# A Mamba block with a mixture of experts on one core: eight of 32 products with C on VectorE, a rearranged prologue, unneeded matmuls behind the loop

## The reference

```python
def _selective_scan(x, dt, Bm, Cm, A, D):
    dA = jnp.exp(dt[..., None] * A)
    dBx = (dt * x)[..., None] * Bm[:, :, None, :]
    def step(h, inputs):
        dA_t, dBx_t, C_t = inputs
        h = dA_t * h + dBx_t
        y = jnp.einsum('bdn,bn->bd', h, C_t)
        return (h, y)
    ...
    return jnp.swapaxes(ys, 0, 1) + x * D[None, None, :]

def _mamba_dir(h, in_proj_w, conv_w, conv_b, x_proj_w, dt_proj_w, dt_proj_b, A_log, D, out_proj_w):
    xz = h @ in_proj_w.T
    x, z = (xz[..., :D_INNER], xz[..., D_INNER:])
    x = jax.nn.silu(_causal_depthwise_conv(x, conv_w, conv_b))
    x_dbl = x @ x_proj_w.T
    dt = jax.nn.softplus(x_dbl[..., :DT_RANK] @ dt_proj_w.T + dt_proj_b)
    ...
    y = _selective_scan(x, dt, Bm, Cm, A, D)
    return (y * jax.nn.silu(z)) @ out_proj_w.T
...
x = x + _L0_attn_ref(_L0_cond_ref(x, cond_8, ...), ...)       # forward and reversed direction
x = x + _L0_ffn_ref(_L0_cond2_ref(x, cond_8, ...), ...)       # top 2 of 8 experts, hidden size 1024
```

## Time and profile before

| | us |
|---|---|
| median of 3 runs | 1420.53 (1418.15 to 1420.72) |
| the profiled execution | 1421.41 |
| its span, first to last instruction | 1419.6 |
| prologue, up to DVE's first scan | 46.9 |
| loop, up to DVE's last gates | 46.9 to 936.3 |
| behind the loop, up to the first expert matmul | 936.3 to 985.4 |
| experts | 985.4 to about 1405 |

### The profile page before, as it was taken

One profiled execution on the slowest core, in us unless ns is written; L12 is line 12 of the kernel. 1 busy time (PEld: TensorE's weight loads), 2 busy tenths in 40 slices (PEclk: granted clock), 3 DMA queues, 4 the chain that ended last, 5 costly groups with the idle time before them and its releaser, 6 DMA issues. The chain is left out here.

```text
span 1419.6 us, 16570 instructions
## 1 busy us (share of the span) xinstructions
PE 1309.1 (92%) x5272; PEld 782.0 (55%) x5272; DVE 948.1 (67%) x1164; ACT 715.8 (50%) x1263; POOL 963.3 (68%) x508
## 2 busy tenths in 40 slices
PE   7898999899998889899897888899999999999997
PEld 3343333343433333333343333346999999999996
DVE  3798999999999999999999999963111111111110
ACT  3887876687776576777677564401111111111111
POOL 1898999999999999999999999824122222222211
PEclk9999999999999999999999999987999999999999
DMA  5554555554555454555555554507889888888882
GB/s 181 187 164 133 177 170 158 165 164 164 164 179 178 147 175 153 169 182 166 170 178 178 172 179 148 186 5 268 305 322 317 319 308 324 313 311 321 321 316 45
DMA packets 105497, 290.33 MB, mean 205 GB/s; under 512 B 9649, under 2 KB 19506, under 8 KB 89922
## 3 DMA queue, kind: packets, MB, share of 16 engines
q1 hardware_dynamic: 95762, 271.17, 54.8%
q0 software_dynamic: 9648, 18.09, 6.3%
HBM read 271.41 MB, written 9.96 MB: 198 GB/s over the span
## 5 line engine op out<-in xcount | busy, mean ns | idle before, releaser
L433 PE MATMUL ps_y<-arena,ident 128*128 128x512 f32 x1024 | 501.9, 621 | 58.1 <-POOL arena L1147 46.1
L1147 POOL TENSOR_TENSOR arena<-arena 128x1024 f32<-128x1024 f32 x184 | 438.4, 2392 | 37.4 <-DVE arena L892 21.6
L433 PEld LDWEIGHTS ps_y<-arena,ident 128*128 128x128 f32 x1024 | 191.6, 196 | 330.2 <-issue 212.3
L1131 POOL TENSOR_TENSOR arena<-arena 128x1024 f32<-128x1024 f32 x128 | 305.3, 2386 | 6.3 <-issue 4.2
L700 ACT ACTIVATE ps_de<-arena,An 128x512 f32<-128x512 f32 x256 | 176.4, 689 | 237.3 <-DVE arena L889 236.4
L1197 POOL DMA_INDIRECT out_x<-arena x39 | 61.8, 1584 | 319.4 <-ACT arena L830 285.1
L876 DVE TENSOR_TENSOR ps_u<-ps_du,arena 128x512 f32<-128x512 f32 x256 | 178.7, 698 | 25.6 <-DVE arena L903 11.2
L1098 DVE TENSOR_TENSOR arena<-ps_du,arena 128x512 f32<-128x512 f32 x39 | 27.0, 692 | 232.9 <-PE ps_du L585 232.9
L700 ACT ACTIVATE arena<-arena,An 128x512 f32<-128x512 f32 x256 | 181.1, 707 | 0.0
L889 DVE TENSOR_TENSOR_SCAN arena<-ps_de,hlast,arena 128x512 f32<-128x512 f32 x128 | 163.1, 1274 | 0.2 <-ACT arena L700 0.2
L889 DVE TENSOR_TENSOR_SCAN arena<-ps_de,arena 128x512 f32<-128x512 f32 x128 | 155.3, 1214 | 6.6 <-ACT arena L700 3.7
(11 more groups left out here) (213 smaller groups left out, 1508.2 us busy)
## 6 DMA issues: line engine op xcount, KB each, us to landing
arena<-bc_scratch SPq DMA_DIRECT2D x256, 512.0 KB, 4.6
arena<-in_W SPq DMA_DIRECT2D x117, 1024.0 KB, 8.1
arena<-arena POOLq DMA_DIRECT2D x15, 512.0 KB, 4.6
arena<-in_xT SPq DMA_DIRECT2D x2, 1024.0 KB, 5.1
arena<-in_w2c SPq DMA_DIRECT2D x1, 2048.0 KB, 8.6
arena<-in_xT SPq DMA_DIRECT2D x4, 512.0 KB, 6.1
X_scratch<-stg SPq DMA_DIRECT2D x12, 128.0 KB, 4.8
out_x<-stg SPq DMA_DIRECT2D x12, 128.0 KB, 5.1
```

The source lines that it names most:

```text
L433: t = e.matmul(Y[j][:, :], ident[:, :], hc[:, i % NP, j, :], start=False, stop=(n == 15))
L1131: e.tensor_tensor(uA[:, turn % 2, :, :], duA.rearrange("p (o t) -> p o t", o=1).to_broadcast([128, 2, TH]), ring[:, turn % NR, 0, :, :], A ...
L1147: e.tensor_tensor(hc[:, i % NP, :, :], hh[:, i % NH, :, :], c, ALU.mult).then_inc(gp_hc, 1)
```

## The change

- **OWN** has eight entries in place of nine, evenly four apart, all at odd units.
- **Prologue.** PE does five matmuls on zeros (128x256, into a free bank) before the first real one. DVE writes the second of the two X tiles, ACT the first. ACT takes exp(A_log) before the step width in place of behind its exp, does ln of the second tile first (`first_ln`), and makes the convolution's diagonals behind the second unit's decays in place of ahead of the first's. DVE adds dt's first tile, POOL the second. POOL's first u is cut in two halves with a semaphore each, so that DVE's first scan waits for one half. DVE's first `second_weights` stands behind its first u.
- **End of the loop.** PE does the first half of the second output block ahead of the last two adds in place of behind them.
- **Behind it.** One unneeded matmul of 512 columns ahead of the logits, one of 256 behind each of the four, one of 512 behind these; four in place of three ahead of the mask matmuls, six in place of four behind them.

```diff
-OWN = (3, 7, 10, 14, 17, 21, 24, 28, 31)
+OWN = (3, 7, 11, 15, 19, 23, 27, 31)
...
         ac_dc = sem("dc")
+        dv_dt, gp_u0 = sem("ddt"), sem("gu0")
         ac_dgD, pe_D, ac_ev = (sem(n) for n in ("dgD", "D", "ev"))
...
             if k < 2:
-                e.wait_ge(gp_dt, k + 1)
+                e.wait_ge(gp_dt if k else dv_dt, 1)
             else:
...
+            e.wait_ge(gp_dz, 1)
+            for _ in range(5):
+                e.matmul(PS[7][:, 0:C], xp[:, 0, PAD:PAD + 128], xp[:, 0, PAD:PAD + C], start=True, stop=True)
             e.wait_ge(l_w0, W0)
...
                     side_work(i)
+                if i == NU:
+                    out_block(1, 0, 1, both_side, (0, 1))
                 if i >= LAG:
...
-            out_block(1, 0, 1, both_side, (0, 1))
             for k in (2, 3):
...
                         t.then_inc(full[2 + c], 1)
+            def warm(n, p=7, w=2):
+                for _ in range(n):
+                    e.matmul(PS[p][:, 0:w * C], ident[:, :], opT[:, 0:w, :].rearrange("p k o -> p (k o)"), start=True,
+                             stop=True)
+            for p in (6, 7):
+                e.wait_ge(freed[p], turns[p])
+            warm(1)
             for i in range(4):
...
                 e.matmul(PS[p][:, 0:E], ones_r, bgr, start=False, stop=True).then_inc(full[p], 1)
-            def warm(n):
-                for _ in range(n):
-                    e.matmul(PS[5][:, :], ident[:, :], opT[:, 0:2, :].rearrange("p k o -> p (k o)"), start=True,
-                             stop=True)
+                warm(1, w=1)
+            warm(1)
...
                 e.wait_ge(freed[p], turns[p])
-            warm(3)
+            warm(4, 5)
             e.wait_ge(gp_rw, 1)
...
             t.then_inc(pe_inv, 1)
-            warm(4)
+            warm(6, 5)
...
                     e.activation(sc1[:, j, :], sc1[:, j, :], ACT.Exp, scale=-1.0).then_inc(ac_se, 1)
+            def first_ln():
+                e.wait_ge(ac_se, 2)
+                for j in (1, 0):
+                    e.activation(sc1[:, j, :], sc1[:, j, :], ACT.Ln, bias=1.0).then_inc(ac_ln, 1)
...
             e.wait_ge(l_x0, WX)
-            x1(0, 0)
+            for m in range(2):
+                is_full(e, ("x1", 0, m, 0))
+            p = place["x1", 0, 0, 0][0]
+            e.activation(X[0][:, 0, HB[0]], PS[p][:, :], ACT.Identity, bias=bb[:, 0:1]).then_inc(freed[p], 1)
             e.wait_ge(l_w, W1)
...
             x_rows(0, 0)
+            e.activation(An[:, :, :, :], Al[:, :, :, :], ACT.Exp).then_inc(ac_A, 1)
             for m in range(2):
...
             step_exp(0, 0, 0)
-            e.activation(An[:, :, :, :], Al[:, :, :, :], ACT.Exp).then_inc(ac_A, 1)
-            step_ln(0, 0, 0)
-            for m in range(2):
-                conv_diag(0, m)
+            first_ln()
             e.wait_ge(dv_An, 1)
...
                 decay(i)
+                if i == 1:
+                    for m in range(2):
+                        conv_diag(0, m)
                 if i >= 2 and unit(i - 2)[1] == 0:
...
                 e.wait_ge(ac_dA, i + 1)
-                e.wait_ge(gp_u, i // 2 + 1)
+                if i == 0:
+                    e.wait_ge(gp_u0, 1)
+                else:
+                    e.wait_ge(gp_u, i // 2 + 1)
                 if i >= NH:
...
                                 ALU.add).then_inc(dv_wm, 1)
+            e.wait_ge(l_x0, WX)
+            p = is_full(e, ("x1", 0, 1, 0))
+            e.tensor_scalar(X[0][:, 1, HB[0]], PS[p][:, :], bb[:, 1:2], None, ALU.add).then_inc(freed[p], 1)
             for m in range(4):
...
                     first_conv(m, k)
-            second_weights(0)
             e.wait_ge(ac_A, 1)
             e.tensor_scalar(An[:, :, :, :], An[:, :, :, :], -1.0, None, ALU.mult).then_inc(dv_An, 1)
+            e.wait_ge(ac_sp, 1)
+            e.wait_ge(ac_ln, 2)
+            e.tensor_tensor(dt[:, 0, :], dt[:, 0, :], sc1[:, 0, :], ALU.add).then_inc(dv_dt, 1)
             for p in range(2, 4):
...
                 u(i)
+                if i == 0:
+                    second_weights(0)
                 scans(i)
...
         def _(e):
-            def first_width(m):
-                e.wait_ge(ac_sp, m + 1)
-                e.wait_ge(ac_ln, m + 1)
-                e.tensor_tensor(dt[:, m, :], dt[:, m, :], sc1[:, m, :], ALU.add).then_inc(gp_dt, 1)
...
                     e.wait_ge(dv_sA, 2 * turn - 2)
+                if turn == 0:
+                    for j, done in enumerate((gp_u0, gp_u)):
+                        e.tensor_tensor(uA[:, 0, j, :], duA, ring[:, 0, 0, j, :], ALU.mult).then_inc(done, 1)
+                    return
                 e.tensor_tensor(uA[:, turn % 2, :, :], duA.rearrange("p (o t) -> p o t", o=1).to_broadcast([128, 2, TH]),
...
-            for m in range(2):
-                first_width(m)
+            e.wait_ge(ac_sp, 2)
+            e.wait_ge(ac_ln, 1)
+            e.tensor_tensor(dt[:, 1, :], dt[:, 1, :], sc1[:, 1, :], ALU.add).then_inc(gp_dt, 1)
             u(0)
```

## The result

The change takes 1405.65 us, median of four runs (1401.53, 1403.74, 1407.56, 1408.77), against 1420.22 us before (four runs, 1418.15 to 1420.72): a ratio of 0.9895, 95% interval 0.9877 to 0.9912. The profiled execution of the change is the one of 1403.74 us (span 1401.9), 17.7 us under the profiled one of before. The forecast was 1400 us, with a range of 1395 to 1411. The trace of the change is thus of an execution 1.9 us under its median.

The account below looks back on a forecast made before the run. DVE was taken to bound the loop, with POOL close behind. From the profiled execution, 1421.4 - 3.0 - 2.8 - 7.3 - 7.9 = 1400.4 us, 1399.5 against the median, stated as 1400; range 1395 to 1411 us.

Parts of the forecast that it names:

- rival 1: Behind the loop: PE's clock falls all the same among the logits, +0.4 in place of -7.9 us; 1408.7 us, chance 0.28.
- First part: Prologue up to the convolution's start: early matmuls raise PE's clock, bias writes run side by side; -3.0 us, bounds -0.6 to -3.6.
- rival 3: Prologue: the early matmuls do not raise PE's clock; 1402.8 us, chance 0.06.
- Second part: Prologue up to DVE's u of unit 1: less work before the first scan; -2.8 us, bounds -1.5 to -4.
- DVE's add beside POOL's: Prologue: DVE's add and du take turns with POOL's; first scan some 0.6 us later than side by side, still in time.
- Loop, -7.3 forecast: Loop: DVE drops its ninth product in eight groups of 32 units, 8 x 0.91 = -7.3 us.
- together 0: Loop: POOL's bumps, about +3 us, and DVE's shorter waits for PE's adds, about -3 us, cancel.
- the +3 for POOL: Loop: POOL's added products, +8.6 us in all, sometimes make DVE wait; about +3 us, bounds 0 to +8.6.
- The -3 for the adds: Loop: DVE's 8.1 us of waits for PE's adds shrink, unit 21 being owned no more; about -3 us, bounds -8.1 to 0.
- Rival 4: Loop: owned unit 19 of every 32 waits 4.1 us for the first add after Y is emptied; 1433 us, chance 0.02.
- Behind the loop, -7.9 forecast: After the loop: unneeded matmuls hold the clock at 2.4 GHz; logits +0.7, L559 -6.7, then +0.6, first tile -1.8 us.
- Rival 2: Loop: POOL becomes the bound, its +8.6 us of added products coming through whole; 1409 us, chance 0.09.

Follow-up runs that it names:

- change_again: The change itself, unaltered, measured once more on another chip beside other variants: 1404.17 us, ratio 0.9892 to the kernel before.
- change_nine: The change with the old list of nine own products in place of eight (new prologue and new end kept): 1405.44 us, ratio 0.9894 to the kernel before.

## Why the prediction was right, and where it was not

The time, 1405.65 us, lies in the range, 5.65 us over the forecast, and between the forecast and rival 1; faster was right. In the pair of traces the sum was -17.7 and not -21.0 us, and 3.1 of the missing 3.3 us are the loop's. The rest, the 1.9 us by which the change's median lies over its trace, has no trace of its own. Measured alone each of the three parts fell short, by 1.6, 4.7 and 2.1 us; that the whole came nearer than their sum is not explained, and two terms came near for the wrong reason. Point by point:

- **Prologue, -5.8 forecast, -5.6 in the trace, -4.2 measured alone.** That the trace came so near is partly luck. First part: -2.3, not -3.0; the sum put x's landing at about 8.6, and L306 waited for it until 9.76 (9.06 to 10.91 in other runs), so the projection began at 14.45, not 13.2. Its main term, the half rate of the passes on x (1.7 us), can't be credited to the early matmuls: without them these passes ran at full rate in three traces of four, with them in seven of ten. In the other three (rival 3) the eight passes took 5.4 us in place of 3.7, and u(1) lies at 46.1 to 46.5, 1.9 to 2.4 us later than the other seven's average of 44.2. What the early matmuls did do every time is speed up L444, 3.6 to 3.75 us without and 1.9 to 2.5 us with them, so that PE then waits for x and no longer for these weights. In the traces that is worth 0.2 us at the start of the passes on x (9.84 against 10.05 us on average). They take 4.0 to 4.6 us, from 1.11 to at most 5.75, where "1.1 to 5.4" was written for ten times 0.47 us. Second part: -3.3, not -2.8, and about the same in every trace.
- **DVE's add beside POOL's.** Both rows end 0.55 us after POOL's: L993 at 38.31 against L1195's 37.76, L887 at 39.98 against L1149's 39.43. So the two took turns, as the Trainium skill (SBUF — State Buffer, "Who interferes with whom") says, and still in time.
- **Loop, -7.3 forecast, -4.2 in the pair of traces, -2.6 measured alone.** The term of the engine's work holds to within 1 us: 870.9 to 862.6 us in the pair, 870.4 to 862.6 on average. The step that failed is "together 0" for POOL's bumps and DVE's waits: in the pair the waits rose from 16.3 to 20.4 us. Of its two halves, the +3 for POOL was 0, since the change's DVE waits for POOL nowhere in the loop. The -3 for the adds was +0.7 in the pair, and in the five traces with this list these waits are 8.8 to 15.1 us where the old list has 8.1 to 11.1. And the waits for anything else had no term at all, though they were 8.2 us of the 16.3: they are 6.3 to 8.2 us with nine and 9.9 to 11.6 us with eight (ACT, the last gates). The bounds "-8.1 to 0" were the mistake: they had no room for a rise, though the prediction itself said that 19 stands where 21 was left.
- **Rival 4 (unit 19's wait) was real but once:** 4.6 us at unit 19, 0.7 at 51, and under 0.3 at 83 and later. Its place was right and its price of eight waits was not. The same chain at place 3 of a block costs as much where the clock is down (4.8 to 5.2 us in three traces).
- **Behind the loop, -7.9 forecast, -7.6 in the trace, -5.8 measured alone.** Logits chain +0.2 (forecast +0.7); L571's end -7.3 against the last gates (forecast -6.7); from there to the first `gu` +1.3 (forecast +0.6); first tile -1.6 (forecast -1.8). The last term was not the fillers': its first `gu` took 5.5 us in the trace of before alone, and 3.9 us in all thirteen others, three of them with the old end. So the near fit of the trace's -7.6 us is luck in this term, and its 1.6 us are most of what the median lacks.
- **Rival 1 (the clock falls all the same)** would fit the first four times, two near 1402.6 and two near 1408.2 us, which the five of change_again don't repeat. At the end it is refuted: ten of ten traces with fillers keep 1.00 there. Where the profiled executions with this list differ most, the clock was down ahead of a new sum in the loop. Of the change's own executions of 1407.56 and 1408.77 us no trace exists, so for them this is argued, not shown.
- **Rival 2 (POOL the bound)** is refuted with eight: DVE waits for it nowhere, and with four buffers the list of nine, which gives POOL less, is slower. With seven, POOL's idle time in the loop (878.8 - 855.8 = 23 us) has come down to DVE's waits (21.8), so there the question is open.

What stays open: why the three parts alone sum to -12.6 us and together give -14.6 to -16.6, and why change_nine's median is that of the change although nine products cost 2.6 us in the kernel before and 3.4 us with four buffers. Both are of the size of the intervals. Why the clock fell on the passes on x in three executions with early matmuls is open too.

## What to carry to other kernels

Moving work off the busiest engine gives its full duration only if that engine waits for nothing; count for each of its waits whether it gets longer when the engine comes sooner, and give such a term bounds on both sides. Where a product or tile waits for a buffer that is freed by a chain across three engines, one more buffer (8 us here) was worth more than any placing of the work (1 to 5 us) or less work (0 to 3 us). Take a small term from several traces of one kernel: two terms here were for 1.4 and 1.6 us the chance of one execution, and both looked like an effect of the change until other traces of the old code were read.

## What the runs showed of the hardware that was not expected

The granted clock of one stretch of identical code was 0.57 in one execution and 0.86 in another, and what that costs depends on the slack of the buffers there: 4.8 us or nothing. The first eight passes on x ran in 3.7 us in three of four traces without early matmuls and in seven of ten with them, and in 5.4 us in the others. The load of x, always issued at 3.09 or 3.10 us, landed between 8.6 and 10.8 us. And matmuls of 256 and 512 columns with unneeded results, 4.7 us of them among the logits, kept the clock at 1.00 through the small matmuls behind the loop in each of ten traces.
